# A fused conditioning layer: the first of sixteen periods rearranged

## The reference, cut to what matters

```python
def _ln(x, g, b):
    m = jnp.mean(x, -1, keepdims=True)
    v = jnp.mean((x - m) ** 2, -1, keepdims=True)
    return (x - m) * rsqrt(v + 1e-5) * g + b
def _mlp_ln(s, W1, b1, W2, b2, g, b):
    return _ln(silu(s @ W1 + b1) @ W2 + b2, g, b)

# x [8, 1024, 512]; ids per token: pathway of 500, kind of 5, scale of 3
h = _ln(_ln(x, pw_g[pathway], pw_b[pathway]), cp_g[kind], cp_b[kind])
t = _ln(x, tm_g[kind], tm_b[kind])
s = _ln(x, ms_g[scale], ms_b[scale])
m, n, r = (x + _mlp_ln(state, ...)[:, None, :] for state in (cond_512, cond_64, fside))
w = softmax(aw)
cat = concatenate([w[0]*h, w[1]*t, w[2]*m, w[3]*n, w[4]*r, w[5]*s], -1)
x = x + _mlp_ln(cat, int_W1, int_b1, int_W2, int_b2, int_g, int_be)   # int_W1 [3072, 512]
styles = cond_512 @ (affine_w / 16).T + affine_b
dcoefs = rsqrt(sum((weight[None] * styles[:, None, :]) ** 2, 2) + 1e-8)
y = clip((x * styles[:, None, :]) @ weight.T * dcoefs[:, None, :] + bias, -256, 256)
return x + y
```

## Time and profile before

| | us |
|---|---|
| median of 3 runs | 1263.73 (1261.84 to 1264.38) |
| profiled execution | 1263.24 |
| its span, first to last instruction | 1261.5 |
| mean granted TensorE clock, share of full | 0.986 |
| TensorE busy | 1214.6 (96%) |
| VectorE busy | 945.0 (75%) |
| ScalarE busy | 542.1 (43%) |
| GpSimd busy | 213.2 (17%) |

### The profile page before, as it was taken

How to read it: one execution, slowest core, us unless ns; L and a number is a source line. 1 busy time by engine, 2 the same in 40 slices (tenths; PEclk the granted TensorE clock), 3 DMA queues, 4 the chain that set the end, 5 groups by cost and what they waited for, 6 DMA issues and landing times.

```text
span 1261.5 us, 15273 instructions
## 1 busy us (share of the span) xinstructions
PE 1214.6 (96%) x5308; PEld 957.0 (76%) x5308; DVE 945.0 (75%) x1754; ACT 542.1 (43%) x836; POOL 213.2 (17%) x262
## 2 busy tenths in 40 slices
PE   4798999999999999999999999999999999999996
PEld 2556887878788787878878787887878788787884
DVE  6776786868878686887868688786868878686836
ACT  3325336353443635344363534436353443635352
POOL 2311120212112021210301121030212103021000
PEclk9898899999999999999999999999999999999998
DMA  9823141232314123231422323142232314222001
GB/s 291 321 77 112 34 142 57 84 98 92 114 35 142 57 84 99 92 109 41 135 64 75 107 92 108 41 134 65 76 107 92 109 39 137 65 76 92 26 2 66
DMA packets 51932, 119.44 MB, mean 95 GB/s; under 512 B 6416, under 2 KB 6800, under 8 KB 51760
## 3 DMA queue, kind: packets, MB, share of 16 engines
q1 hardware_dynamic: 37520, 68.12, 16.9%
q0 software_dynamic: 14336, 50.34, 12.3%
HBM read 101.66 MB, written 16.78 MB: 94 GB/s over the span
## 4 chain that ended last, share of the span: by engine, by line
PE 49%; DVE 28%; issue 9%; ACT 6%; DMA 6%; POOL 1%; SPq 0%; DVEq 0%; POOLq 0%
PE pre L1045 10%; PE pre L1049 10%; PE pre L1052 9%; DMA gc<-cp_table,k_ids 4%; PE uy L1094 4%; PE uy L1095 4%; PE uy L1097 4%; DVE ug L753 3%; DVE lo_b L710 3%; DVE lo_a L760 3%; PE turn L1024 3%; ACT tmp_c L451 2%; PE turn L1008 2%; DVE raw L626 2%; DVE gb L649 2%
## 5 line engine op out<-in xcount | busy, mean ns | idle before, releaser
L423 ACT ACTIVATE gb<-gb,ra 128x512 f32<-128x512 f32 x64 | 46.3, 724 | 222.9 <-DVE gb L662 209.4
L354 POOL DMA_INDIRECT gb<-pw_table,pw_ids x64 | 67.9, 1061 | 399.3 <-PE turn L1008 382.6
L1094 PE MATMUL uy<-hi_c,w_hi_w 128*128 128x512 f32 x256 | 107.0, 418 | 4.7 <-ACT hi_c L453 4.1
L1097 PE MATMUL uy<-lo_c,w_hi_w 128*128 128x512 f32 x256 | 106.8, 417 | 0.2
L1107 PE MATMUL uy<-hi_a,w_hi_l 128*128 128x512 f32 x256 | 101.1, 395 | 4.7 <-ACT hi_a L481 4.7
L1110 PE MATMUL uy<-lo_a,w_hi_l 128*128 128x512 f32 x256 | 101.3, 396 | 0.7 <-DVE lo_a L760 0.7
L1095 PE MATMUL uy<-hi_c,w_lo_w 128*128 128x512 f32 x256 | 101.0, 394 | 0.0
L1108 PE MATMUL uy<-hi_a,w_lo_l 128*128 128x512 f32 x256 | 100.8, 394 | 0.0
L1077 PE MATMUL pre<-lo_b,w_hi_x 128*128 128x512 f32 x256 | 99.6, 389 | 0.0
L1076 PE MATMUL pre<-hi_b,w_lo_x 128*128 128x512 f32 x256 | 99.6, 389 | 0.0
L1075 PE MATMUL pre<-hi_b,w_hi_x 128*128 128x512 f32 x256 | 99.6, 389 | 0.0
(11 more groups left out here) (204 smaller groups left out, 2896.2 us busy)
## 6 DMA issues: line engine op xcount, KB each, us to landing
xT<-x_turned SPq DMA_DIRECT2D x64, 256.0 KB, 2.8
out_turned<-xT SPq DMA_DIRECT2D x64, 256.0 KB, 2.0
xt<-x_in SPq DMA_DIRECT2D x62, 256.0 KB, 2.6
sel_in<-sel_ids SPq DMA_DIRECT2D x16, 192.0 KB, 2.4
raw_t<-int_w SPq DMA_DIRECT2D x1, 1024.0 KB, 7.1
raw_s<-int_w SPq DMA_DIRECT2D x1, 1024.0 KB, 11.4
gb<-pw_table,pw_ids POOLq DMA_INDIRECT x64, 5.1
raw_h<-int_w SPq DMA_DIRECT2D x1, 1024.0 KB, 19.5
```

The lines of the kernel that those rows point to most:

```text
L1094: pe.matmul(bank, w_hi["w2"][:, c, cut], hi["c"][:, c, :], start=c == 0, stop=False)
L1097: last = pe.matmul(bank, w_hi["w2"][:, c, cut], lo["c"][:, c, :], start=False, stop=c == C - 1)
```

## The change

Only the first period and the first part of the second are written anew; the loop from the second period on is the same except for three insertions.

- **Start.** On VectorE the softmax of `aw` goes behind the statistics of all four x tiles. Eight small early loads move from SP's to ScalarE's queue: identity, `cmp`, `aw`, `tab_t`, the first chunk of `w_t`, both id arrays, `cols`. The identity gets 32 more columns (`fold`), which VectorE no longer adds up.
- **Weights by chunk.** `w_t` is loaded, split high and low in four chunks, `w_s` loaded in two and split in four; TensorE waits per chunk. The chunks of `w_t` go between those of x turned in SP's queue.
- **h weight and table rows.** ScalarE multiplies `raw_h` by its factor in place (`h_scaled`), then four highs; the four lows go to GpSimd (`low_h_weights`), as does the low part of the table rows.
- **Early fetches.** The gathers of tiles 0 to 3 get places of their own (`gc_stage`, `gb_stage` in room that is free by then), so seven of the eight go out at once, without waiting for the styles or a second norm.
- **Styles in the first MLP layer.** `mlp_first` computes them as a fourth strip of 32 output rows beside the three MLPs (6 pieces of 512 columns, all with 128 partitions); the 8 products of `style_cols` and their turn bank are gone. They are turned with the MLP's hidden rows.
- **Order on TensorE.** Gains of s and turns of h move to other places; the second MLP layer stands ahead of turns 2 and 3 of h; turning `c` and the batch rows stand ahead of and behind the fourth unit of h; table, batch columns, offsets and demodulation stand between x units.
- **Offset table.** The moving weights are used once for high and low rows, which stand side by side (64 output rows): 24 matmuls; VectorE adds the two halves after a ScalarE copy.
- **Demodulation.** Four matmuls of 512 columns into four strips of 32 rows, a ScalarE copy, four small products with `fold` (`demod_rows`, `demod_cols`). Its root is taken in the second period, and the high and low part of `l1` are made there, the low part on GpSimd in one 128x2048 operation.
- **x weight sum.** The order of summands is r, m, n (was m, n, r), in other room; loads of `w_m`, `w_n`, `w_w2` wait for the room.

The diff, cut to its core:

```diff
-    uses = [("rows", 0)] + [("gt", 0, c) for c in range(3)]
...
+    uses = [("rows", 0)] + [("gt", 0, c) for c in range(4)] + [("gs", 0, c) for c in range(3)]
+    uses += [("h", 0, 0), ("gs", 0, 3), ("h", 0, 1), ("mlp_h",), ("h", 0, 2), ("h", 0, 3)]
+    uses += [("mlp_c",), ("batch",), ("dsum",), ("rows", 1), ("dcoef",)] + [("gt", 1, c) for c in range(3)]
...
+            load_xT(0, 0)
+            for c in range(1, C):
+                put_part("t", 1, c)
+                load_xT(0, c)
             put("tab_s", tab_raw["s"], tab_src[1])
+            put_part("s", 5, 0)
+            put_part("s", 5, 1)
...
+            sp.wait_ge(mlp1_mm, 1)
+            put("w_r", wr_in, w1_part(4))
             put("b2", b2_in, b2_row.rearrange("(a d) -> a d", a=1).to_broadcast([P, D]))
             load_xt(4)
             load_xt(5)
+            sp.wait_ge(q_done, 3)
+            put("w_m", wm_in, w1_part(2))
             sp.wait_ge(mlp2_mm, 1)
             put("w_w2", raw_w["w2"], square(int_w2))
+            sp.wait_ge(turn_filled, use_of["h", 0, 3] + 1)
+            put("w_n", wn_in, w1_part(3))
...
+            def low_h_weights(c):
+                pool.wait_ge(hi_done["h"], c + 1)
+                nc.gpsimd.tensor_tensor(w_lo["h"][:, c, :], raw_w["h"][:, c, :], w_hi["h"][:, c, :].bitcast(F32),
+                                        ALU.subtract).then_inc(lo_done["h"], 1)
...
+                if i == 1:
+                    pool.wait_ge(hi_done["l1"], 1)
+                    nc.gpsimd.tensor_tensor(w_lo["l1"][:].rearrange(flat), raw_w["l1"].rearrange(flat),
+                                            w_hi["l1"][:].bitcast(F32).rearrange(flat), ALU.subtract).then_inc(lo_done["l1"], 1)
...
+            def high(n, c, scale):
+                act.wait_ge(w_loaded[n][c * len(w_loaded[n]) // C], 16)
+                nc.scalar.activation(w_hi[n][:, c, :], raw_w[n][:, c, :], ACT.Copy, scale=scale).then_inc(hi_done[n], 1)
...
+                if i == 1:
+                    dve.wait_ge(dco_in, 1)
+                    inverse_root(small[:, 1], dcoef[:], small[:, 0], link, dco_ready)
+                    dve.wait_ge(dco_ready, 1)
                 find_root(i - 1)
...
+                for m, (k, w, last_one) in enumerate(((0, w1_in[:, 0, :], False), (2, w1_in[:, 2, :], True), (3, w1_in[:, 2, :], True),
+                                                      (0, aff_raw[:, 0, :], False))):
+                    pe.matmul(uy[QUAD * m:QUAD * (m + 1), 0, :], mx[:, k, :], w, start=True, stop=last_one)
...
-                        pe.matmul(uy[0:QUAD, 1, :], row_hi[:, k, c, :], w_lo[n][:, c, :], start=False, stop=False)
-                        last = pe.matmul(uy[0:QUAD, 1, :], row_lo[:, k, c, :], w_hi[n][:, c, :], start=False,
...
+                        pe.matmul(uy[0:2 * QUAD, 1, :], row_split[:, k, c, :], w_hi[n][:, c, :], start=k == 0 and c == 0, stop=False)
...
+                for c in range(C):
+                    last = pe.matmul(bank[QUAD * c:QUAD * (c + 1), :], sstyle[:, c, :], squares[:, c, :], start=True, stop=True)
```

More of the change, by code:

```diff
@@ L400, in _ @@
                     gather_gb(f + 2)
-                if not i:
-                    pool.wait_ge(c_var, 1)
-                    nc.gpsimd.tensor_tensor(crow[0:TROWS, 3:4], crow[0:TROWS, 2:3], half[0:TROWS, :], ALU.pow).then_inc(c_rs, 1)
-                    rstd_x(f)
-                if more:
                     rstd_x(f + 1)
@@ new lines, in _ @@
+            split_s(0, 3)
+            act.wait_ge(w_loaded["h"][0], 16)
+            nc.scalar.activation(raw_w["h"], raw_w["h"], ACT.Copy, scale=wsm[:, 0:1]).then_inc(h_scaled, 1)
+            act.wait_ge(h_scaled, 1)
+            for c in range(C):
+                high("h", c, 1.0)
+            split_h(0, 1)
+            act.wait_ge(ld["row"], 16)
+            nc.scalar.activation(row_hi, row_raw.rearrange("p (n c r) -> p n c r", n=3, c=C), ACT.Copy).then_inc(row_hi_done, 1)
+            gate(2)
@@ new lines, in _ @@
+            gate(4)
+            act.wait_ge(bias_ready, 1)
+            hidden(0, 0)
+            act.wait_ge(ld["w_l1"], 16)
+            nc.scalar.activation(squares, raw_w["l1"], ACT.Square).then_inc(l1_sq, 1)
+            hidden(0, 1)
+            hidden(0, 2)
+            filled(act, "batch")
+            nc.scalar.activation(mh, filled(act, "dsum"), ACT.Copy).then_inc(dsum_copied, 1)
+            hidden(0, 3)
+            split_rows(1)
+            gate(5)
+            act.wait_ge(b2_ready, 1)
@@ L513, in _ @@
+            filled(act, "dcoef")
+            u_out(0, 0)
+            split_t(1, 0)
+            u_out(0, 1)
+            add_be(0, 0)
+            split_t(1, 1)
+            add_be(0, 1)
+            u_out(0, 2)
+            add_be(0, 2)
+            add_be(0, 3)
+            gate(6)
+            for i in range(1, GROUPS):
+                n, more = i + 1, i + 1 < GROUPS
+                u_out(i - 1, 3)
+                split_t(i, 2)
+                split_sum(i - 1)
                 split_t(i, 3)
-                if not i:
-                    gate(0)
-                    act.wait_ge(ld["w_s"], 16)
-                    high("s", raw_w["s"], wsm[:, 5:6])
@@ L1067, in offsets, with first_offsets @@
                 last.then_inc(b_used, 1)
+            def first_offsets():
+                pe.wait_ge(tab_ready["b"], 1)
+                for o in range(C):
+                    last = pe.matmul(pre[:, o, :], tab["b"][:, o * P:(o + 1) * P], rows[:], start=False, stop=o < 2)
+                    if o < 2:
+                        last.then_inc(pre_ready, 1)
+                last.then_inc(b_used, 1)
             def unit_x(i, o):
```

718 lines of the change are left out of this document (381 added, 337 removed).

## The result

The changed kernel took 1244.92 us (median of 4 runs, 1241.96 to 1246.38), the one before 1263.12 (4 runs, 1261.84 to 1264.38); the ratio is 0.9853 with a 95% interval of 0.9832 to 0.9874. The forecast was 1240, so the direction is right and the time lies in the range of 1231 to 1254; of the 23 us of gain that were forecast, 18 to 19 came and 5 are missing. The profiled execution took 1244.63 us.

What follows compares the result with a forecast made beforehand. TensorE, busy 96% of the span, was taken as the bound, with time to win in the first period's holes and slow clock. 1263.24 - 30.9 + 1.0 + 2.5 + 2.2 + 1.8 = 1239.8 us, median 1240, range 1231 to 1254.

Steps and rivals of the forecast that it cites:

- Start: First period's beginning: row pick at about 11.5, first unit from 21.23 to about 15.9, 5.3 us gained; queue move costs nothing.
- VectorE's stretch and TensorE beside it: First period: last low part of s at 42.4, low h3 at 54.6, first h unit 53.0 to 58.3 at half clock.
- Shorter pieces: First period: table 5.6 us, MLP layers 1.8 and 3.6, demodulation 1.8; second period's first unit at 102.9 instead of 131.24.
- Handing over and hold: First period: 1.0 us for handing over between engines and 2.5 for GpSimd holding VectorE, added to 102.9.
- rival of late transfers: Early loads and MLP weights: start's gain lost, or 3 us waiting plus 2.6 of half clock; 1246 us, chance 0.13.
- GpSimd's queue: Rival: roots for gates 2, 3 and 7 wait behind GpSimd's moved work; loses from 5.4 us a chunk; chance 0.05.
- the 28 us: Gain of 28.3 us forecast at the second period's first unit, from the first period's new order, before handing over and holds.
- Work moved to GpSimd: Low parts on GpSimd, 1.5 us a chunk and 4.6 for 2048 columns; about half holds VectorE: 2.5 and 2.2 us.
- 2.2 us in the second: Second period: VectorE's loss to GpSimd's 2048-column operation, taken as about half of its 4.6 us.
- full-hold rival: VectorE stands for all 4 x 1.5 and 4.6 us, plus 2.6 of half clock in the second period; 1248, chance 0.2.
- Root: Demodulation's root, eight small VectorE steps before find_root in the second period; with 0.3 us of slack, 1.8 us lost.
- 1.00 us row: Profile row: GpSimd's 128x1 power took 1.00 us, not 0.56, under a VectorE operation with both inputs in SBUF.

Runs made afterwards that it cites:

- loads on SP: Changed kernel with the eight early loads put back from ScalarE's queue to SP's, in the old places; median 1244.24 us.
- root late: Changed kernel with the demodulation's root moved from ahead of find_root to behind all_x1 in the second period; median 1242.24 us.

## Why the prediction was right, and where it was 5 us off

**Start.** Forecast: row pick 11.5, first unit 15.9. Measured 11.46 and 16.02; 5.2 us gained of 5.3. The forecast gave all of it to the order and nothing to the queue, and the run with the loads on SP bears that out (16.13).

**VectorE's stretch and TensorE beside it.** Without the hold, forecast: last low part of s 42.4, second norm(2) 46.6, last s unit's end 45.3, first h unit 53.0 and 5.3 us long. Measured: 42.0, 46.6, 45.5, and 54.58 to 59.84. That 42.4 was met is in part luck. The first unit's clock rose before its end, so it ended at 20.48 and not at 21.2, and VectorE made the tile of gain t3 at 20.91, not at 22.0; but it then waited 2.58 us for gain s3, where the forecast had 1.3. Low h3 was done at 56.6, against 54.6 plus the 2.5 of hold. The hold itself was 2.6 us, as shown above.

**Shorter pieces.** Table 5.6 us (72.41 to 77.97), first MLP layer 1.8 (30.48 to 32.3), second 3.6 (46.27 to 49.8), the demodulation's products 1.8 (88.11 to 89.1 and 92.41 to 93.2), all as forecast; second period's first unit at full clock, as forecast. Handing over and hold made the second period start 2.2 us behind 102.9, not 3.5: 1.3 us to the good, which is no more than its scatter between runs. The waits for transfers were 0.7 and 0.8 us; the rival of late transfers stayed small. So did that of GpSimd's queue: the root for gate 3 began at 51.20, after GpSimd had been idle for 1.76 us behind the chunks, and that for gate 7 at 134.94, after 9.91 us. These parts of the 28 us were read from the trace of the changed kernel and agree with the forecast one by one; of the first period only the start, the place of the h weight's low parts and the last hole were switched by themselves in a run.

**Work moved to GpSimd.** The durations taken, 1.5 and 4.6 us, were right (3.06 and 3.10 for a pair of chunks, 4.60 for 2048 columns; the 4.5 of the Trainium skill's GPSIMD Engine Reference, 3.1, Elementwise, agrees too). For the chunk that holds only of the time that passed: one took 1.29 us (44.53) where VectorE did not hold it, and 1.42 to 1.82 where it first had to wait for a VectorE step with both inputs in SBUF.

**The step that failed** is the term "2.2 us in the second", from "Between nothing and the whole 4 x 1.5 and 4.6 us I take about half": it measured 4.3 us, and the 2.5 us of half clock that come with it were not in the sum. In these runs the hold is not a share. A VectorE instruction with both inputs in SBUF, or the `TENSOR_SCALAR` on 512 columns, stands until GpSimd's operation ends; one with an input in PSUM, or the statistics, does not stand at all. So the hold has to be read from what VectorE does at that moment. In the first period the steps beside the chunks are mixed (subtractions with a PSUM input, statistics, short ones), and 2.6 us were held of 7.2 (four chunks and the row part). In the second, `find_root` is eight steps in a row within SBUF, and 4.3 of 4.6 us were held. The forecast named the place ("before find_root") and the slack (0.3 us) for the root, and did not use them for GpSimd's operation, though its own terms of 2.2 and 1.8 us already made a hole of some 4 us there. With 4.3 for 2.2, and 2.5 us of half clock, for which the full-hold rival had 2.6 at this very place, the sum is 1239.8 + 2.1 + 2.5 = 1244.4. So the rival was right in the second period and the forecast in the first, where half was a guess that came out, and the rival's 1248 was too high because it held the first period's 6 us whole. The rest, 0.5 us in the second period (a turn waiting for a low part), 1 us of scatter later and the 1.3 us to the good, cancels, which is luck.

**Root.** 1.8 us forecast; 1.7 measured on the period's length, 1.82 on the hole.

## What to carry to other kernels

In these runs, work moved from VectorE to GpSimd was free only beside VectorE instructions that read PSUM or do statistics, or where VectorE waited; beside a chain within SBUF it cost nearly its full length (4.3 of 4.6 us), and the clock behind the hole as well. Decide by what VectorE's timeline shows in the stretch where the operation will run, and look first for idle VectorE time that can take the operation itself: there 128x512 costs 0.6 to 0.7 us, on GpSimd 1.3 to 1.8. And when a hole of the bounding engine is filled, look up what the next due input is before counting the gain: here VectorE was next at once.

## What the runs showed that was not expected

- Idling of 3.17 us ahead of the turn of h in the second period left the granted clock full; 4.59 and 4.99 us in the same place brought a unit at half clock (2.06 us for four matmuls).
- In the first period 2.4 to 3.6 us of idling ahead of the last turn of h brought half clock in every profile with that hole but one, and for different lengths: 5.3 us in the changed kernel (54.58 to 59.84), 3.3 with the root late (54.13 to 57.46), none with the loads on SP, where the h units behind a hole of 2.42 us took 1.16 us from the start. Two other profiles with the same 2.42 us had half clock. What decides between them was not tried and stays open, so the 2.5 us of clock in the sum is what these rows show and no rule for other holes.
- GpSimd is held by VectorE as well, and longer than the forecast's 1.00 us row suggested: its 128x1 power took 2.52 us at 64.85, under VectorE's 128x2048 step with both inputs in SBUF (64.61, 2.34 us), instead of 0.56.
